# One exponential over four score banks in place of two over two banks each, in the attention of a layer with attention and mixture of experts

## The reference

```python
xn = layernorm(x)                                   # x: (8, 2048, 1024)
x  = x + attn(xn) + ffn(xn)
# attn: 16 heads of 64; q, k, v and the output projection have rank 32:
#   holo_linear(x) = (x @ basis.T) @ (amp * cos(phase)).T
attn = softmax(einsum('bhqd,bhkd->bhqk', q, k) * 64 ** -0.5)
out  = einsum('bhqk,bhkd->bhqd', attn, v)
# ffn: 8 experts (top 2 of a softmax gate, hidden 1408) and a shared one (hidden 2816),
#   each silu(x @ wg) * (x @ wu) @ wd; the experts are computed for all tokens
#   and weighted with a (token, expert) table
```

## Time and profile before

| | us |
|---|---|
| two timed runs | 4249.7 and 4642.7 |
| their median | 4446.2 |
| the profiled execution, whole | 4264.7 |
| its span, on core 4, the slowest | 4263.1 |
| spans of its cores | 4237.5 to 4263.1 |

### The profile page before, as it was taken

The page is one execution under the profiler, slowest core; times in us unless marked ns, Lnnn a source line. Parts: engine busy times, 40 slices in busy tenths (PEclk is TensorE's granted clock), DMA queues, the critical chain, the costliest instruction groups (busy, mean ns, idle before and its releaser), DMA issues.

```text
span 4263.1 us, 47768 instructions; the slowest of 8 cores (4237.5 to 4263.1 us)
## 1 busy us (share of the span) xinstructions
PE 3303.3 (77%) x13711; PEld 1257.9 (30%) x13923; DVE 1820.7 (43%) x2757; ACT 1001.3 (23%) x1377; POOL 267.5 (6%) x351
## 2 busy tenths in 40 slices
PE   2224536666666646999999999999999999999996
PEld 1111101111111112334333333343433334433432
DVE  4332253333333343544444445444445544344334
ACT  1333316666666601001101100111100011100110
POOL 1000000000000001011000000110000110000100
PEclk9998558888888857999988999999999999999995
DMA  1100000000000005224322222352222244222404
GB/s 33 30 30 1 1 0 1 1 1 1 1 1 1 1 10 60 30 30 50 40 30 30 30 30 30 34 55 31 31 30 30 32 44 45 30 30 30 45 1 149
DMA packets 254451, 116.18 MB, mean 27 GB/s; under 512 B 233592, under 2 KB 233592, under 8 KB 254208
## 3 DMA queue, kind: packets, MB, share of 16 engines
q0 software_dynamic: 245248, 87.87, 19.2%
q1 hardware_dynamic: 8960, 25.24, 1.9%
HBM read 191.40 MB, written 8.39 MB: 47 GB/s over the span
## 4 chain that ended last, share of the span: by engine, by line
PE 67%; ACT 14%; DVE 9%; issue 8%; DMA 1%; DVEq 1%; ACTq 1%; POOL 0%; SPq 0%; POOLq 0%
PE p_d L826 19%; PE p_xu L793 18%; PE p_xg L784 18%; ACT pTs L610 11%; PE p_st L599 4%; PE p_a L580 2%; PE p_t L336 1%; PE p_b L580 1%; DMA out<-o 1%; DVE acc L834 1%; DVE gbuf L808 1%; PE p_a L468 1%; DVE v_aug L507 1%; PE p_vt L500 1%; DVE acc L691 1%
## 5 line engine op out<-in xcount | busy, mean ns | idle before, releaser
L826 PE MATMUL p_d<-gbuf,wdbuf 128*128 128x512 bf16 x3449 | 842.6, 383 | 96.9 <-DVE gbuf L816 44.2
L784 PE MATMUL p_xg<-xnh_fm,wgbuf 128*128 128x512 bf16 x3449 | 844.9, 386 | 29.8 <-DMA wdbuf<-w_down 25.2
L793 PE MATMUL p_xu<-xnh_fm,wubuf 128*128 128x512 bf16 x3450 | 838.0, 383 | 4.1 <-issue 0.2
L803 ACT ACTIVATE sgt<-p_xg 128x512 bf16<-128x512 f32 x440 | 262.7, 597 | 2237.9 <-PE p_xg L784 1772.0
L834 DVE TENSOR_TENSOR acc<-acc,p_d 128x512 f32<-128x512 f32 x896 | 616.6, 688 | 302.3 <-PE p_d L826 295.2
L808 DVE TENSOR_TENSOR gbuf<-sgt,p_xu 128x512 bf16<-128x512 bf16 x440 | 302.4, 687 | 996.1 <-PE p_xu L793 966.4
L610 ACT ACTIVATE pTs<-p_st,bias 128x1024 bf16<-128x1024 f32 x512 | 570.6, 1114 | 353.3 <-PE p_st L599 297.0
L784 PEld LDWEIGHTS p_xg<-xnh_fm,wgbuf 128*128 128x128 bf16 x3520 | 348.3, 99 | 455.9 <-issue 68.5
L826 PEld LDWEIGHTS p_d<-gbuf,wdbuf 128*128 128x128 bf16 x3520 | 286.6, 97 | 653.0 <-issue 455.7
L793 PEld LDWEIGHTS p_xu<-xnh_fm,wubuf 128*128 128x128 bf16 x3520 | 347.8, 99 | 426.8 <-issue 36.3
L599 PE MATMUL p_st<-q_fm,k_fm 64*128 64x512 bf16 x1024 | 277.6, 442 | 247.9 <-ACT pTs L610 247.2
(11 more groups left out here) (209 smaller groups left out, 1179.7 us busy)
## 6 DMA issues: line engine op xcount, KB each, us to landing
wgbuf<-w_gate POOLq DMA_DIRECT2D x88, 256.0 KB, 13.6
wubuf<-w_up POOLq DMA_DIRECT2D x88, 256.0 KB, 14.5
wdbuf<-w_down POOLq DMA_DIRECT2D x88, 256.0 KB, 15.0
x_tm<-x SPq DMA_DIRECT2D x16, 512.0 KB, 3.5
x<-x SPq DMA_DIRECT2D x16, 512.0 KB, 4.5
out<-o SPq DMA_DIRECT2D x16, 512.0 KB, 5.3
wgbuf<-sw_gate POOLq DMA_DIRECT2D x22, 256.0 KB, 10.5
wubuf<-sw_up POOLq DMA_DIRECT2D x22, 256.0 KB, 11.2
```

The lines of the kernel that those rows point to most:

```text
L784: emit("tensor", lambda te, buf=buf, loc=loc, c=c, tg=tg: te.matmul(p_xg[:, :], wgbuf[buf][:, loc * 1024 + c * 128: loc * 1024 + c * 128 + ...
L793: emit("tensor", lambda te, buf=buf, loc=loc, c=c, tg=tg: te.matmul(p_xu[:, :], wubuf[buf][:, loc * 1024 + c * 128: loc * 1024 + c * 128 + ...
L803: emit("scalar", lambda s, ss=ss: s.activation(sgt[ss][:], p_xg[:, :], AF.Silu), waits=[("t", t_xg), sgt_free[ss]], incs=[("s", 1)])
L826: first=(li == 0), last=(li == len(grp) - 1): te.matmul(pb[:, :], wdbuf[buf][:, li * 1024 + dc * 128: li * 1024 + dc * 128 + 128], gbuf[bu ...
```

## The change

The two exponentials of a part become one of 128x2048 over all of `p_st`. It waits for all four score matmuls, and the first of the next part's four waits for it. Order and number of the matmuls are unchanged, and so are the parts of `pTs`. `st_half_free` is gone; `st_free` takes its place.

```diff
-    st_half_free = {0: list(st_free), 1: list(st_free)}
...
             if pair < 8:
                 pp = pair % 2
-                t_sp = {}
+                first = True
...
-                            waits=(st_half_free[sidx] if j == 0 else []) +
-                                  ([("v", v_bias)] if (mi == 0 and pair == 0 and
-                                                       sidx == 0 and j == 0) else []),
+                            waits=(st_free if first else []) +
+                                  ([("v", v_bias)] if (mi == 0 and pair == 0 and first)
+                                   else []),
                             incs=[("t", 1)])
-                        t_sp[sidx] = cnt["t"]
-                for sidx in (0, 1):
-                    emit("scalar", lambda s, pp=pp, sidx=sidx: s.activation(
-                        pTs[:, pp * 2048 + sidx * 1024: pp * 2048 + sidx * 1024 + 1024],
-                        p_st[:, sidx * 1024: sidx * 1024 + 1024], AF.Exp,
-                        scale=0.125, bias=bias128[:]),
-                        waits=[("t", t_sp[sidx]), pTs_free[pp]], incs=[("s", 1)])
-                    st_half_free[sidx] = [("s", cnt["s"])]
+                        first = False
+                t_sp = cnt["t"]
+                emit("scalar", lambda s, pp=pp: s.activation(
+                    pTs[:, pp * 2048: pp * 2048 + 2048],
+                    p_st[:, 0:2048], AF.Exp,
+                    scale=0.125, bias=bias128[:]),
+                    waits=[("t", t_sp), pTs_free[pp]], incs=[("s", 1)])
+                st_free = [("s", cnt["s"])]
                 exp_done[pair] = cnt["s"]
```

## The result

The changed kernel takes 0.978 of the time before (95% interval 0.9754 to 0.9806), 2.2% less; the interval reaches from 1.9 to 2.5%. The profiled execution went from 4264.7 to 4151.9 us. The median of the timed runs is 4177.7; some timed runs of either kernel were disturbed, which lifts medians, and the ratios leave them out. The forecast was 4203 in a range of 4160 to 4275, and within 2%.

What follows compares the result with a forecast made beforehand. Only the attention stage could move: 871.5 of 4263.1 us, 570.6 exponentials, the rest mostly ScalarE waiting for scores. Terms -54 - 67 + 60 = -61, checked as minus 62, took 4264.7 to 4203 us, range 4160 to 4275.

Steps and rivals of the forecast that it cites:

- The longer exponential: ScalarE in attention: one exponential of 1965 ns replaces two of 1114, 256 times; minus 67 us.
- The gaps inside a part: ScalarE in attention: the gap between a part's two exponentials goes; minus 54 us, leaving 2 us of excess.
- The lost overlap: Between parts: all four score matmuls follow the exponential, gaps 0.90 for 0.70, 1.34 for 0.91 at half clock; plus 60 us.
- Pairing after a stall: Score matmuls after an exponential: they run in pairs; a gap of 1.1 at full clock would disprove it.
- AV and VectorE's copies: TensorE behind the scores: AV stays hidden; at a step's start its margin over VectorE's copies shrinks but holds.
- 64 of 224 gaps at half clock: Gaps between parts inside a step: 64 stay at half clock, adding 64 x 0.43 us to the sum.
- between two steps nothing changes: Passage from one attention step to the next: 31 gaps stay at 73 us.
- the stretch without AV: Step's beginning, where parts 0 and 1 have no AV and TensorE does only scores; forecast to get 0.45 us shorter.
- rival A: Attention: the clock falls less often; 44 us more saved if it no longer fell, 4159 us; chance 0.14.
- Rival B: Attention: longer TensorE idle stretches keep the clock low; 95 us more, 4298 us; chance 0.08.
- Rival C: Attention: the longer exponential saves nothing; at 2228 ns the sum is +6, 4270 us; chance 0.06.
- Within 2%: Whole kernel: time changes by no more than 2%, 85 us, about what a measurement can tell; chance 0.82.

Runs made afterwards that it cites:

- e3: The changed kernel with the two 128x1024 exponentials of before put back, scores still in one burst; profiled 4302.0 us, stage 922.8 us.
- e2: The changed kernel with one extra ScalarE copy after the exponentials of parts 2 to 7; profiled 4244.2 us, stage 868.7 us.
- e6: The kernel before, with parts numbered through over all steps so no stretch lacks AV; ratio to before 0.987.
- e9: The changed kernel with two extra ScalarE copies after part 0's exponential in each step; profiled 4186.8 us, stage 808.0 us.
- e4: The kernel before, with score matmuls ordered A0, A1, B0, B1 in place of A0, B0, A1, B1; ratio to before 0.975.
- e7: The kernel before, with score order A0, A1, B0, B1 and parts numbered through over all steps; ratio to before 0.964.
- e5: The changed kernel with parts numbered through over all steps so no stretch lacks AV; ratio to before 0.971.
- e8: The changed kernel with one extra ScalarE copy after the exponentials of parts 3 and 5 only; ratio to before 0.984.
- e11: The kernel before, with score order A0, A1, B0, B1, parts numbered through and two more PSUM banks for AV; ratio to before 0.955.

## Why the prediction was wrong

The mechanism of the change came out as written; the clock did not. By the steps of the sum:

- *The longer exponential*: 1967 ns against 1965 taken, 256 times; minus 67.0 us against minus 67. The Trainium skill (ScalarE: Activation LUTs, What ACT_TABLE_LOAD costs) puts it at about 1990, 1.2% above the trace.
- *The gaps inside a part*: gone. Eight exponentials have 0.28 more ahead of them, as one at 911.16 with 1.21, half of the sixteen of before, as assumed.
- *The lost overlap*: gap 0.92 at full clock against 0.90 (4 us in all), and 1.34 at half clock as forecast; e3 shows its price alone, 50 us against the 60 of the sum. Pairing after a stall holds, four matmuls in 0.60 to 0.61 us.
- *AV and VectorE's copies*: AV stays hidden at full clock; AV of part 0 starts 2.65 us after the step's first exponential, the value of the working (1.97 + 0.15 + 0.53).
- *The failed step: "64 of 224 gaps at half clock", and "between two steps nothing changes", 73 us.* Both carried the clock of before over. The forecast had 304 to 305 us of gaps, measured were 272.4. The 31 gaps between steps were all 1.89 us, 58.6 in place of 73: minus 14. The other 18 lie inside the steps, where 201 of 224 gaps are at 0.92 on this core. 808 - 32 = 776. What the runs showed in place of the old clock: it is granted in full for 93% of the stage, because the pace went from 3.13 to 2.89 us and the stretch without AV got 0.41 us shorter (e2, e6, e9).

That is rival A, which had 0.14 and was priced at 44 us when no fall is left; 32 us of it came, with 52 of 261 us at half clock left. Against it I had set that the stretch without AV gets only 0.45 us shorter. The place was right, for all falls that are left begin there; I looked at it alone, and at its length. The pace of the parts, which the same sum had just worked out as 2.87 in place of 3.13, I used for the time but not for the clock; and the argument that the clock had stood at 0.85 through the whole stage says only what it does at the pace of before. Rival B argued from the longer single idle stretch (1.30 us now) that the clock could stay low; e2, where that stretch is 1.59 us, shows how near this was: 417 us at half clock. Rival C fell with the 1967 ns. As to the rule of the Trainium skill cited with it (Perfetto Trace Analysis, Matmuls, rotating through banks): once the order of the matmuls lets the overlap happen, it was worth as much as the longer instruction (e4 0.975, after 0.978), and with the parts numbered through in both a little more (e7 0.964, e5 0.971). On the numbers: the median of 4177.7 lies in the range, the profiled execution's 4151.9 lies 8 us below its lower end. Of the 51 us between 4203 and 4151.9, 32 are those of the stage; the other 19 are what core 4 of before, on whose time the forecast was built, had lost outside attention. Against the timed run of 4249.7 the prediction had 4188, and 0.978 of that run is 4156: again 32. "Within 2%" had 0.82; the measured 2.2% is beyond it, where 0.16 had been put, though its interval reaches back to 1.9%.

## What to carry to other kernels

When a change makes a stage faster while TensorE's work in it stays the same, price the clock anew: look in the trace where in a step the clock falls and how long each fall lasts, take the share at half clock as a term that depends on the pace, and, where the granted clock of before is between its levels, give the two cases (all at full, as before) about equal weight. That weight is my choice after this one case. Before lengthening an instruction to save gaps, ask what each gap waits for in the list of the engine that feeds it: here one matmul stood in the wrong place, and exchanging two loops brought as much as the change, without giving up the overlap on which the faster versions rest.

## What the runs showed that I had not expected

- A delay of 0.29 us in five of the seven gaps of a step took the time at half clock from 52 to 417 us, in two of seven to 88 (e2, e8). At a mean clock of 0.76 the matmuls were the same and in one burst.
- With the stretches without AV gone, half clock was 48, 86 and 132 us at paces of 2.89, 3.13 and 3.35 us; with them 52, 261 and 310. At the slower paces the stretches count for most of it. At the fast pace the like numbers hide two causes: AV's wait for VectorE's copies had come in their place.
- With that wait taken away by two more PSUM banks, at a pace of 2.63 us, no core's clock fell any more in the stage (e11).
- A ScalarE copy of 128x1, put behind an exponential with the wait for its own instruction before it, delays what follows by 0.29 us; two of them by 0.59.
